# One core, six sweeps over a 4096x4096 matrix: another block order in the first sweep, 25 blocks taken whole in place of 32, small work at other places

## The chip, the cores and the metric

One core of a Trainium2 chip runs the whole program. The metric is device time in microseconds from the start to the end of one execution; lower is better. The engines that matter here are TensorE (PE in the profile; PEld is its weight load), VectorE (DVE), ScalarE (ACT), GpSimd (POOL) and SyncE (SP), which only issues transfers.

## The reference, cut to what matters

Six products with the same adjacency matrix `adj` (4096x4096, float32), each between small work on rows of 128 values:

```python
def ref_cut(x, adj, ...):
    deg = clip(sum(adj, axis=1), 1.0)
    x = layernorm(x + x @ W_self + (adj @ x / deg) @ W_neigh)        # sweep 0
    x = layernorm(x + relu(adj @ (x @ kernel) + bias))               # sweep 1
    h = relu(adj @ (x @ W1) + b1)                                    # sweep 2
    x = layernorm(x + relu(adj @ (h @ W2) + b2))                     # sweep 3
    x1 = silu((adj @ x) @ W + b)                                     # sweep 4
    return layernorm(x + silu((adj @ x1) @ W + b))                   # sweep 5
```

## The kernel before

**Tiling.** `adj` is cut into 8x8 blocks of 512x512. A block (r, k) comes in two tiles of 128x1024 float32 (512 KB each); each tile is one *step* of the program. `STEPS` lists them in their order: 516 steps, of which 0 to 129 and a few after are of the first sweep. The step is loaded by SP into one of six buffers `raw` (L434). Use of a step by TensorE is a *product*; `PRODUCTS` lists 768 of them. A product adds into `acc`, a bank of PSUM for one of the 48 sums (`FINISH` numbers the sums m = 0 to 47 in the order in which they end, 8 for each sweep; FINAL is 47).

**Two ways through TensorE.** A *whole* step (`whole_step`, L476) multiplies the raw float32 tile: each float32 matmul of 512 columns is two records in the profile, four records for a step. A *split* step (`split_step`) needs two rounded parts first. ScalarE writes `adj_hi` (a rounding of the tile, L729), VectorE writes `adj_lo` = raw - `adj_hi` (L882), and TensorE does six single-pass matmuls: L488 and L489 twice on `adj_hi`, then L493 twice on `adj_lo`. The operand (`op_hi`, `op_lo`) is split likewise. Parts lie in nine slots (`SPLIT`), with four more in the last sweep, in the space of `op_hi` and `op_lo` of the sweep before; so there the same L729 and L882 write `op_hi` and `op_lo`. A split step can serve two sweeps from one load: in the order table, WHOLE is a whole block, ONE a split block used for one sweep, BOTH for two sweeps at once, and FIRST with a later SECOND for two sweeps at two places. 

**Degrees.** In the first sweep VectorE also adds every tile of `adj` into `deg_part` (L751 for the first pair of a row of blocks, L754 after it), and each sum waits for the one before it, since it reads it. At a row's end it makes `deg_sum` (L759). A raw buffer of a whole step is free for the next load when TensorE and the degree sum have read it; that of a split step when `adj_lo` and the degree sum are made.

**Small work of the first sweep,** for each sum m. TensorE: `degrees` (L511) puts the row sums across partitions, `rows_of_x` (L503) makes x @ (W_self + I), `times_weight` (L525) multiplies the finished sum by the weight. VectorE: L807 and L809 clip and invert the degree (`rdeg`; L807 waits for L511), L813 to L770 add and take means and variances (ending in `var_eps`), L847 makes `shift`, L865 the next operand's `op_lo`. GpSimd computes `rstd` = var_eps ** -0.5 (L905) between `var_eps` and `shift`. ScalarE: `sum_out` (L612) copies the finished bank to `t_agg`, L663 scales, L683 normalises into `t_x`, L692 makes `op_hi`.

**In the last sweep,** VectorE adds the bias (L829, waits for L525), ScalarE applies silu (L674), VectorE adds the residual and takes the moments (L842 to L770), GpSimd and L847 follow, ScalarE normalises (L683) and issues the store (L704). The last two steps are worked off in `last_block` (L562, L564, L569) with smaller pieces and a short chain to the end (L619, L537, L632, L780, L909, L797).

**What sets the order.** Nothing is scheduled at run time. Each engine walks through its own list in program order and blocks at a semaphore that is not there yet. The block order is the table `FIRST_ORDER` (and tables for the later sweeps). The place of each piece of small work is a number in a second set of tables. For TensorE (`ROWS_AT`, `DEGREES_AT`, `WEIGHT_AT`) it is the number of the product that it stands before. For ScalarE and VectorE (`SUM_AT`, `NORM_AT`, `SCALE_AT`, `RESIDUAL_AT` and others) it is eight times a step plus a part: a number u stands before the split of step u // 8. An operation that stands early blocks whatever is behind it on its engine.

Of the kernel before, what the change touches and what calls it, by code (L numbers as in the profile page):

```python
# [5 lines left out]
def bass_gnn_residual_norm_kernel(  # L6
# [52 lines left out]
        (0, 1, 0, WHOLE), (0, 0, 0, WHOLE), (0, 1, 1, WHOLE), (0, 0, 1, WHOLE), (0, 1, 5, WHOLE), (0, 0, 7, WHOLE),  # L59
        (0, 0, 5, WHOLE), (0, 1, 4, WHOLE), (0, 0, 4, WHOLE), (0, 0, 3, WHOLE), (0, 0, 6, WHOLE), (0, 0, 2, WHOLE),  # L60
        (0, 1, 2, WHOLE), (0, 1, 3, ONE), (0, 2, 5, WHOLE), (0, 1, 6, WHOLE), (0, 1, 7, WHOLE), (0, 2, 2, WHOLE),
        (0, 2, 6, WHOLE), (0, 2, 3, ONE), (0, 2, 7, WHOLE), (0, 3, 5, WHOLE), (0, 2, 1, WHOLE), (0, 2, 4, WHOLE),
        (0, 2, 0, BOTH), (0, 3, 6, WHOLE), (0, 3, 1, BOTH), (0, 4, 0, BOTH), (0, 4, 4, WHOLE), (0, 3, 2, BOTH),
        (0, 3, 3, ONE), (0, 4, 7, WHOLE), (0, 3, 0, BOTH), (0, 3, 4, ONE), (0, 3, 7, WHOLE), (0, 4, 1, BOTH),
        (0, 5, 0, FIRST), (0, 5, 6, WHOLE), (0, 4, 2, BOTH), (0, 4, 5, WHOLE), (0, 5, 2, BOTH), (0, 4, 3, BOTH),
        (0, 4, 6, WHOLE), (0, 5, 1, FIRST), (0, 5, 0, SECOND), (0, 5, 4, FIRST), (0, 6, 2, FIRST), (0, 5, 1, SECOND),
# [4 lines left out]
        (1, 3, 3, ONE), (1, 2, 2, ONE), (0, 7, 6, SECOND), (0, 6, 5, SECOND)
# [92 lines left out]
    for s, g in enumerate(SPLIT_STEP):  # L164
# [778 lines left out]
```

## Time and profile before

| | |
|---|---|
| median of 3 runs | 1144.3 us (1143.35 to 1145.77) |
| profiled execution, its own time | 1143.78 us |
| its span, first to last instruction | 1141.7 us |
| TensorE busy | 1130.8 us, 99% |
| VectorE busy | 829.4 us, 73% |
| ScalarE busy | 571.9 us, 50% |
| DMA | 278.41 MB, mean 244 GB/s |

Between the span and the execution's own time lie 2.1 us of start and end. Engines run side by side, so their shares don't add up. Matmul records overlap: a record is longer than the distance to the next one. What an instruction costs its engine's queue is therefore read from the distance of two starts in the timeline, or from the chain of work, where each piece is counted from one release to the next.

### The profile page before, as it was taken

The page shows a single profiled execution, that of the slowest core. Times are in us where ns is not written, and L with a number is a line of the kernel's source. Part 1 is how long each engine was busy: PE and PEld are TensorE (multiplying, and loading weights), DVE is VectorE, ACT ScalarE, POOL GpSimd, SP SyncE. Part 2 cuts the span into 40 slices and gives each one's busy share as a digit, 9 for nine tenths or more (in the row PEclk, how much of TensorE's full clock was granted, in tenths as well). Part 3 has the DMA queues.
Part 4 walks back from the last instruction along what each step waited for, and adds up shares of the span by engine and source line. Part 5 has one row for each costly group of instructions (what it writes and reads, how often), then busy time and mean ns, then how long its engine had stood idle before and what let it go on. Part 6 is the DMA issues. An engine that isn't in the chain of part 4 may idle for free.

```text
span 1141.7 us, 14128 instructions
## 1 busy us (share of the span) xinstructions
PE 1130.8 (99%) x5012; PEld 901.1 (79%) x5012; DVE 829.4 (73%) x1089; ACT 571.9 (50%) x669; POOL 72.8 (6%) x49
## 2 busy tenths in 40 slices
PE   8999999999999999999999999999999999999997
PEld 3556677778888888888888888888888888888886
DVE  6898899889898666585544498566678455677887
ACT  1234335435754444474444474444467445566875
POOL 0010000000141111000000010000000000000121
PEclk9999999999999999999999999999999999999999
DMA  9988677666868666596656587666658665797885
GB/s 356 342 287 278 228 251 249 228 220 204 296 210 293 210 193 213 176 345 225 213 184 210 175 297 271 218 199 213 222 200 323 212 206 186 247 330 282 310 277 175
DMA packets 82643, 278.41 MB, mean 244 GB/s; under 512 B 8848, under 2 KB 14480, under 8 KB 82576
## 3 DMA queue, kind: packets, MB, share of 16 engines
q1 hardware_dynamic: 76144, 272.86, 69.7%
q10 hardware_dynamic: 6432, 4.65, 1.4%
q8 instruction: 42, 0.69, 0.2%
q14 instruction: 25, 0.20, 0.0%
HBM read 275.38 MB, written 2.10 MB: 243 GB/s over the span
## 4 chain that ended last, share of the span: by engine, by line
PE 96%; DVE 2%; DMA 1%; ACT 0%; issue 0%; SPq 0%; POOLq 0%; POOL 0%; ACTq 0%; DVEq 0%
PE acc L488 27%; PE acc L493 27%; PE acc L489 27%; PE acc L476 10%; PE acc L525 4%; DMA raw<-adj_tiles 1%; DVE adj_lo L882 1%; PE acc L503 1%; PE acc L511 1%; ACT adj_hi L729 0%; DVE stats L765 0%; ACT t_x L683 0%; DVE t_y L829 0%; DVE op_lo L882 0%; DVE x_rows L852 0%
## 5 line engine op out<-in xcount | busy, mean ns | idle before, releaser
L882 DVE TENSOR_TENSOR adj_lo<-raw,adj_hi 128x1024 fp32r<-128x1024 f32 x431 | 523.3, 1228 | 252.6 <-ACT adj_hi L729 237.2
L729 ACT CAST adj_hi<-raw 128x1024 fp32r<-128x1024 f32 x431 | 450.6, 1051 | 382.5 <-PE acc L493 271.1
L488 PE MATMUL acc<-adj_hi,op_hi 128*128 128x512 f32 x1360 | 537.3, 395 | 0.0
L489 PE MATMUL acc<-adj_hi,op_lo 128*128 128x512 f32 x1360 | 529.7, 390 | 0.0
L493 PE MATMUL acc<-adj_lo,op_hi 128*128 128x512 f32 x1360 | 419.1, 389 | 0.2 <-DVE adj_lo L882 0.2
L493 PEld LDWEIGHTS acc<-adj_lo,op_hi 128*128 128x128 f32 x1360 | 255.2, 188 | 54.2 <-DVE adj_lo L882 0.6
L489 PEld LDWEIGHTS acc<-adj_hi,op_lo 128*128 128x128 f32 x1360 | 255.6, 188 | 53.2 <-issue 1.9
L488 PEld LDWEIGHTS acc<-adj_hi,op_hi 128*128 128x128 f32 x1360 | 255.5, 188 | 53.2 <-issue 1.9
L754 DVE TENSOR_TENSOR deg_part<-deg_part,raw 128x1024 f32<-128x1024 f32 x112 | 136.8, 1222 | 7.0 <-DMA raw<-adj_tiles 3.8
L905 POOL TENSOR_TENSOR rstd<-var_eps,minus_half 128x4 f32<-128x4 f32 x31 | 55.2, 1782 | 1056.2 <-DVE var_eps L770 1056.2
L476 PE MATMUL acc<-raw,x_rows 128*128 128x512 f32 x256 | 115.1, 600 | 4.4 <-DMA x_rows<-x_blocks 4.2
L476 PEld LDWEIGHTS acc<-raw,x_rows 128*128 128x128 f32 x256 | 48.3, 192 | 58.7 <-issue 53.1
L612 ACT COPY t_agg<-acc 128x512 f32<-128x512 f32 x47 | 27.6, 586 | 83.6 <-PE acc L493 70.4
L882 DVE TENSOR_TENSOR op_lo<-raw,op_hi 128x1024 fp32r<-128x1024 f32 x21 | 25.4, 1223 | 12.5 <-ACT op_hi L729 12.1
L525 PEld LDWEIGHTS acc<-w,t_agg 128*128 128x128 f32 x248 | 32.4, 191 | 2.4
L525 PE MATMUL acc<-w,t_agg 128*128 128x128 f32 x248 | 32.6, 274 | 0.0
L683 ACT ACTIVATE t_x<-t_y,shift,rstd 128x128 f32<-128x128 f32 x60 | 24.7, 483 | 12.3 <-DVE shift L847 12.1
L729 ACT CAST op_hi<-raw 128x1024 fp32r<-128x1024 f32 x21 | 21.9, 1049 | 13.8 <-PE acc L493 8.6
L765 DVE BATCH_NORM_STATS2 stats<-t_y 128x6 f32<-128x128 f32 x124 | 27.1, 282 | 1.1
L829 DVE TENSOR_TENSOR t_y<-acc,b 128x512 f32<-128x512 f32 x31 | 21.3, 687 | 7.6 <-PE acc L525 7.6
L852 DVE TENSOR_SCALAR x_rows<-t_y,moments,rstd 128x128 f32<-128x128 f32 x64 | 21.6, 400 | 0.0
L604 ACT CAST op_hi<-x_rows 128x512 fp32r<-128x512 f32 x8 | 4.9, 619 | 29.1 <-DMA x_rows<-x_blocks 29.1
(70 smaller groups left out, 327.0 us busy)
## 6 DMA issues: line engine op xcount, KB each, us to landing
raw<-adj_tiles SPq DMA_DIRECT2D x515, 512.0 KB, 4.8
xt<-x_t ACTq DMA_DIRECT2D x8, 256.0 KB, 4.6
x_rows<-x_blocks SPq DMA_DIRECT2D x7, 256.0 KB, 6.3
out<-t_x ACTq DMA_DIRECT2D x7, 256.0 KB, 4.3
raw<-adj_tiles SPq DMA_DIRECT2D x2, 256.0 KB, 3.4
out<-xt SPq DMA_DIRECT2D x2, 128.0 KB, 2.1
x_rows<-x_blocks SPq DMA_DIRECT2D x1, 192.0 KB, 3.5
w<-W ACTq DMA_DIRECT2D x2, 64.0 KB, 3.3
```

The lines of the kernel that those rows point to most:

```text
L476: last = nc.tensor.matmul(bank, cols(x_rows, k)[:, j * P:(j + 1) * P], raw[:, g % RAW, b * CW:(b + 1) * CW], start=first and b == 0, stop= ...
L488: nc.tensor.matmul(bank, op_block(op_hi, p, j), a_hi, start=first and b == 0, stop=False)
L489: nc.tensor.matmul(bank, op_block(op_lo, p, j), a_hi, start=False, stop=False)
L493: last = nc.tensor.matmul(bank, op_block(op_hi, p, j), split_lo(s)[:, b * CW:(b + 1) * CW], start=False, stop=ends and b == BPT - 1)
L525: last = nc.tensor.matmul(bank[:, b * D:(b + 1) * D], t_agg[:, m % 2, b * P:(b + 1) * P], W_OF[p][:], start=True, stop=True)
L612: nc.scalar.copy(t_agg[:, m % 2, :], acc[:, BANK["sum", m], :]).then_inc(agg_out, 1)
L683: nc.scalar.activation(t_x[:, blk], t_y[:, m % 2, blk], ACT.Identity, bias=shift[:, m % 2, b:b + 1], scale=rstd[:, m % 2, b:b + 1]).then_i ...
L729: nc.scalar.copy(split_hi(s), raw[:, g % RAW, :]).then_inc(hi_ready, 1)
L754: nc.vector.tensor_tensor(sums, sums, src, ALU.add).then_inc(deg_step, 1)
L765: nc.vector.bn_stats(stats[:, m % 2, b, :], t_y[:, m % 2, b * D:(b + 1) * D]).then_inc(stats_ready, 1)
L882: nc.vector.tensor_tensor(split_lo(s), raw[:, g % RAW, :], split_hi(s).bitcast(fp32), ALU.subtract).then_inc(lo_ready, 1)
L905: nc.gpsimd.tensor_tensor(rstd[:, m % 2, :], var_eps[:, m % 2, :], minus_half[:], ALU.pow).then_inc(rstd_ready, 1)
```

## The change

Four things, all in tables; no function is touched.

1. `FIRST_ORDER` is another order of the first sweep's blocks, with 25 blocks WHOLE in place of 32. The other seven are split: 14 steps more, 466 in place of 452. The number of steps (516) and of products (768), and so the loads, stay; from step 134 and product 186 on the steps and products are the same ones.
2. The places of the first sweep's small work follow the new order.
3. In the sweeps between, some small work moves by one or two steps.
4. In the last sweep, bias, residual and moments of most sums stand one to five steps later, and around the end the order on ScalarE and VectorE is another.

The first and last lines of the tables that the prediction speaks of:

```diff
     FIRST_ORDER = [
-        (0, 1, 0, WHOLE), (0, 0, 0, WHOLE), (0, 1, 1, WHOLE), (0, 0, 1, WHOLE), (0, 1, 5, WHOLE), (0, 0, 7, WHOLE),
...
-        (1, 3, 3, ONE), (1, 2, 2, ONE), (0, 7, 6, SECOND), (0, 6, 5, SECOND)
+        (0, 0, 5, WHOLE), (0, 1, 5, WHOLE), (0, 0, 1, WHOLE), (0, 1, 1, WHOLE), (0, 0, 6, WHOLE), (0, 0, 3, WHOLE),
...
+        (0, 7, 6, SECOND)
     ]
...
     DEGREES_AT = [
-        25, 35, 52, 80, 103, 130, 150, 178
+        25, 33, 59, 75, 100, 136, 161, 179
     ]
...
     SUM_AT = [
...
-        3198, 3278, 3374, 3454, 3686, 3830, 3878, 3918, 3958, 3974, 4022, 4094, 4129
+        3198, 3278, 3374, 3454, 3686, 3830, 3878, 3926, 3974, 3998, 4054, 4128, 4131
     ]
     SCALE_AT = [
...
-        None, None, None, None, None, 3901, 3941, 3972, 4006, 4029, 4126, 4131
+        None, None, None, None, None, 3894, 3942, 3996, 4038, 4053, 4110, 4130
     ]
...
     NORM_AT = [
-        254, 334, 462, 630, 742, 894, 974, 1118, 1212, 1222, 1246, 1350, 1430, 1526, 1606, 1702, None, None,
+        238, 318, 518, 598, 726, 902, 1030, 1126, 1220, 1236, 1254, 1350, 1430, 1518, 1598, 1702, None, None,
...
     RESIDUAL_AT = 40 * [None] + [
-        3862, 3894, 3926, 3958, 3974, 4030, 4128, 4129
+        3854, 3902, 3950, 3990, 4006, 4070, 4129, 4131
     ]
```

**VectorE after the first sum of the first sweep, before** (from the moments of m = 0, behind step 27, to step 38; `deg_part` is the running row sum, `shift` waits for GpSimd's `rstd`):

```order
L768 BN_AGGR moments<-stats 128x2 x4
L770 TENSOR_SCALAR var_eps<-moments 128x4
L751 TENSOR_TENSOR deg_part<-raw 128x1024
L754 TENSOR_TENSOR deg_part<-deg_part,raw 128x1024
L847 SCALAR_TENSOR_TENSOR shift<-moments,rstd 128x4
L754 TENSOR_TENSOR deg_part<-deg_part,raw 128x1024 x3
L759 TENSOR_TENSOR deg_sum<-deg_part 128x512
L865 TENSOR_TENSOR op_lo<-t_x,op_hi 128x512
L754 TENSOR_TENSOR deg_part<-deg_part,raw 128x1024 x3
L807 TENSOR_SCALAR rdeg<-acc 128x4
```

The same place with the change (every line number is one higher, since the table is a line longer):

```order
L769 BN_AGGR moments<-stats 128x2 x4
L771 TENSOR_SCALAR var_eps<-moments 128x4
L755 TENSOR_TENSOR deg_part<-deg_part,raw 128x1024
L848 SCALAR_TENSOR_TENSOR shift<-moments,rstd 128x4
L755 TENSOR_TENSOR deg_part<-deg_part,raw 128x1024 x3
L760 TENSOR_TENSOR deg_sum<-deg_part 128x512
L866 TENSOR_TENSOR op_lo<-t_x,op_hi 128x512
L752 TENSOR_TENSOR deg_part<-raw 128x1024
L883 TENSOR_TENSOR adj_lo<-raw,adj_hi 128x1024
L808 TENSOR_SCALAR rdeg<-acc 128x4
```

What moved: between `var_eps` and `shift` stands one degree sum in place of two, and the next split comes four steps sooner.

**ScalarE at the end of the program, before** (the last four steps' splits; `t_agg<-acc 128x512` is the copy of the sum m = 46, `t_x` the normalisation, `128x256` the pieces of the last block):

```order
L612 COPY t_agg<-acc 128x512
L729 CAST op_hi<-raw 128x1024 x2
L729 CAST adj_hi<-raw 128x1024 x2
L683 ACTIVATE t_x<-t_y,shift,rstd 128x128 x4
L704 DMA out<-t_x 128x4x128
L729 CAST adj_hi<-raw 128x1024
L674 ACTIVATE t_aux<-t_y 128x512
L619 COPY t_agg<-acc 128x256 x2
L632 ACTIVATE t_aux<-acc 128x256
L624 COPY t_agg<-acc 128x256
L632 ACTIVATE t_aux<-acc 128x256
L683 ACTIVATE t_x<-t_y,shift,rstd 128x128 x4
```

With the change:

```order
L684 ACTIVATE t_x<-t_y,shift,rstd 128x128 x4
L705 DMA out<-t_x 128x4x128
L730 CAST adj_hi<-raw 128x1024 x3
L613 COPY t_agg<-acc 128x512
L675 ACTIVATE t_aux<-t_y 128x512
L684 ACTIVATE t_x<-t_y,shift,rstd 128x128 x4
L705 DMA out<-t_x 128x4x128
L620 COPY t_agg<-acc 128x256 x2
L633 ACTIVATE t_aux<-acc 128x256
L625 COPY t_agg<-acc 128x256
L633 ACTIVATE t_aux<-acc 128x256
```

What moved: the normalisation of m = 45 stands before the last three splits and no longer between them; the copy of m = 46 stands behind the last split in place of five splits ahead of it; the normalisation and store of m = 46 stand before the copies of the last sum and not at the very end. TensorE's order at the end did not change: its `times_weight` of m = 46, which waits for that copy, is still before product 762, six products from the end.

## Rows read from the trace of the kernel before

**Rows 1.** The page, parts 1 and 2: busy time of engines; TensorE's clock over the span.

```profile
PE 1130.8 (99%) x5012; PEld 901.1 (79%) x5012; DVE 829.4 (73%) x1089; ACT 571.9 (50%) x669; POOL 72.8 (6%) x49
...
PEclk9999999999999999999999999999999999999999
```

**Rows 2.** TensorE's waits from 320 us on: us in total, times, longest.

```profile
PE acc L569 <- DVE adj_lo L882: 0.5, 1, 0.5
PE acc L562 <- ACT adj_hi L729: 0.3, 1, 0.3
PE acc L493 <- DVE adj_lo L882: 0.2, 1, 0.2
```

**Rows 3.** The chain of work, 50 to 111 us: start, us, what.

```profile
50.21 0.79 PE acc L511 x8
51.00 1.82 PE acc L476 x4
52.82 0.89 PE acc L525 x8
...
56.03 0.45 PE acc L493 x2
...
83.39 10.30 PE acc L476 x24
...
108.00 0.45 PE acc L493 x2
...
109.36 0.45 PE acc L493 x2
```

**Rows 4.** VectorE's timeline, 51 to 58 us: start, us, engine, line, operation.

```profile
51.04 0.16 DVE L807 TENSOR_SCALAR rdeg<-acc 128x4 f32<-128x4 f32 x1 [3.79 <-PE acc L511]
...
51.33 1.20 DVE L882 TENSOR_TENSOR adj_lo<-raw,adj_hi 128x1024 fp32r<-128x1024 f32 x1
52.44 1.22 DVE L754 TENSOR_TENSOR deg_part<-deg_part,raw 128x1024 f32<-128x1024 f32 x1
53.58 1.22 DVE L882 TENSOR_TENSOR adj_lo<-raw,adj_hi 128x1024 fp32r<-128x1024 f32 x1
...
55.84 0.69 DVE L813 TENSOR_TENSOR t_y<-t_y,t_aux 128x512 f32<-128x512 f32 x1
...
57.89 0.17 DVE L770 TENSOR_SCALAR var_eps<-moments 128x4 f32<-128x4 f32 x1
```

**Rows 5.** VectorE's timeline, 60 to 66 us.

```profile
60.66 3.88 DVE L754 TENSOR_TENSOR deg_part<-deg_part,raw 128x1024 f32<-128x1024 f32 x3
64.57 0.69 DVE L759 TENSOR_TENSOR deg_sum<-deg_part 128x512 f32<-128x512 f32 x1
65.18 0.68 DVE L865 TENSOR_TENSOR op_lo<-t_x,op_hi 128x512 fp32r<-128x512 f32 x1
```

**Rows 6.** Timeline, 78 to 81 us: moments of m = 1, GpSimd, shift.

```profile
78.25 0.17 DVE L770 TENSOR_SCALAR var_eps<-moments 128x4 f32<-128x4 f32 x1
...
80.45 0.16 DVE L847 SCALAR_TENSOR_TENSOR shift<-moments,rstd 128x4 f32<-128x4 f32 x1 [0.90 <-POOL rstd L905]
```

**Rows 7.** VectorE's waits, 1065 to 1112 us: us in total, times, longest.

```profile
DVE t_y L829 <- PE acc L525: 3.5, 4, 1.5
DVE t_y L842 <- ACT t_aux L674: 2.3, 3, 1.0
```

**Rows 8.** Timeline of ScalarE at the end.

```profile
1120.69 0.59 ACT L612 COPY t_agg<-acc 128x512 f32<-128x512 f32 x1 [0.23 <-PE acc L493]
...
1127.45 1.65 ACT L683 ACTIVATE t_x<-t_y,shift,rstd 128x128 f32<-128x128 f32 x4
...
1129.61 1.05 ACT L729 CAST adj_hi<-raw 128x1024 fp32r<-128x1024 f32 x1 [0.51 <-ACT t_x L683]
...
1132.51 0.65 ACT L619 COPY t_agg<-acc 128x256 f32<-128x256 f32 x2 [1.32 <-PE acc L569]
```

**Rows 9.** Timeline of TensorE at the end.

```profile
1123.21 1.05 PE L525 MATMUL acc<-w,t_agg 128*128 128x128 f32 x8
```

More of the change, by code:

```diff
@@ L69, in bass_gnn_residual_norm_kernel @@
-        (0, 6, 1, FIRST), (0, 6, 7, WHOLE), (0, 6, 0, BOTH), (0, 7, 0, BOTH), (0, 6, 1, SECOND), (0, 6, 4, SECOND),
-        (0, 7, 3, BOTH), (0, 7, 5, BOTH), (0, 7, 6, FIRST), (0, 7, 7, ONE), (0, 7, 2, BOTH), (0, 7, 1, BOTH),
-        (1, 3, 3, ONE), (1, 2, 2, ONE), (0, 7, 6, SECOND), (0, 6, 5, SECOND)
+        (0, 0, 5, WHOLE), (0, 1, 5, WHOLE), (0, 0, 1, WHOLE), (0, 1, 1, WHOLE), (0, 0, 6, WHOLE), (0, 0, 3, WHOLE),
+        (0, 1, 3, WHOLE), (0, 1, 6, WHOLE), (0, 0, 2, WHOLE), (0, 0, 4, WHOLE), (0, 0, 0, WHOLE), (0, 0, 7, WHOLE),
@@ new lines, in bass_gnn_residual_norm_kernel @@
+        (0, 1, 4, WHOLE), (0, 1, 7, ONE), (0, 1, 0, WHOLE), (0, 1, 2, WHOLE), (0, 2, 3, WHOLE), (0, 3, 3, ONE),
+        (0, 3, 7, WHOLE), (0, 2, 7, WHOLE), (0, 2, 5, ONE), (0, 2, 1, WHOLE), (0, 2, 4, ONE), (0, 2, 6, WHOLE),
+        (0, 3, 5, WHOLE), (0, 2, 2, WHOLE), (0, 3, 1, BOTH), (0, 2, 0, BOTH), (0, 3, 6, ONE), (0, 4, 4, WHOLE),
+        (0, 3, 4, ONE), (0, 3, 0, BOTH), (0, 4, 5, WHOLE), (0, 3, 2, BOTH), (0, 4, 1, BOTH), (0, 4, 7, ONE),
+        (0, 4, 6, WHOLE), (0, 5, 5, ONE), (0, 4, 0, BOTH), (0, 4, 2, BOTH), (0, 5, 0, FIRST), (0, 4, 3, BOTH),
@@ new lines, in bass_gnn_residual_norm_kernel @@
+        (0, 5, 3, FIRST), (0, 5, 0, SECOND), (0, 6, 2, BOTH), (0, 6, 3, FIRST), (0, 5, 1, BOTH), (0, 5, 4, BOTH),
+        (0, 6, 4, FIRST), (0, 5, 3, SECOND), (0, 5, 2, BOTH), (0, 5, 6, ONE), (0, 6, 1, FIRST), (1, 4, 4, ONE),
+        (0, 5, 7, ONE), (0, 6, 4, SECOND), (0, 6, 3, SECOND), (0, 6, 7, ONE), (0, 7, 2, FIRST), (0, 7, 3, FIRST),
+        (0, 6, 1, SECOND), (0, 6, 0, FIRST), (0, 7, 2, SECOND), (0, 7, 3, SECOND), (0, 6, 6, ONE), (0, 7, 0, BOTH),
+        (0, 6, 5, FIRST), (0, 7, 4, FIRST), (0, 6, 5, SECOND), (0, 7, 7, ONE), (0, 7, 5, BOTH), (0, 7, 1, FIRST),
@@ L72, in bass_gnn_residual_norm_kernel @@
+        (0, 6, 0, SECOND), (1, 2, 2, ONE), (0, 7, 6, FIRST), (0, 7, 1, SECOND), (0, 7, 4, SECOND), (1, 3, 3, ONE),
+        (0, 7, 6, SECOND)
     ]
@@ L174, in bass_gnn_residual_norm_kernel @@
     ROWS_AT = [
-        21, 31, 42, 59, 88, 111, 138, 158
+        21, 31, 39, 66, 82, 108, 143, 168
     ]
     DEGREES_AT = [
-        25, 35, 52, 80, 103, 130, 150, 178
+        25, 33, 59, 75, 100, 136, 161, 179
     ]
     WEIGHT_AT = [
-        26, 37, 54, 83, 106, 133, 153, 180, 194, 198, 202, 220, 238, 260, 278, 304, 318, 322, 326, 348, 366,
-        388, 406, 432, 446, 450, 454, 476, 494, 516, 534, 560, 574, 578, 582, 604, 622, 644, 662, 702, 720, 726,
-        732, 738, 742, 750, 762, 768
+        26, 34, 61, 77, 103, 138, 163, 181, 194, 198, 202, 220, 238, 260, 278, 304, 318, 322, 326, 348, 366,
+        388, 406, 432, 446, 450, 454, 476, 494, 516, 534, 560, 574, 579, 582, 604, 622, 644, 662, 702, 720, 726,
+        732, 738, 742, 751, 762, 768
     ]
```

31 lines of the change are left out of this document (11 added, 20 removed), and 16 rows, old and new, of tables (BIAS_AT, NORM_AT, SCALE_AT, SUM_AT).

## The prediction, made before the changed kernel ran

> **What bounds the kernel now.** I read the page's busy shares first. TensorE is busy 99% of the span and its clock stands at full speed (2.4 GHz) throughout [rows 1]. Then the waits: from 320 us to the end TensorE waits 1.0 us in all, 0.8 us of it at the last block [rows 2], and in the first sweep only for its first operands. So TensorE's own work sets the time, almost everywhere. What shortens that work shortens the kernel, as long as no wait appears in its place. The question is whether VectorE, which pays for the exchange, can keep up in the first sweep.
>
> **What a step costs TensorE.** In the chain, 24 records of whole matmuls, six steps, take 10.30 us: 1.717 us a step [rows 3]. A split step is the distance between two L493 pairs in a row, 109.36 - 108.00 = 1.36 us [rows 3]; 1.361 over longer runs. A step that goes from whole to split saves 0.356 us. Fourteen do: **14 x 0.356 = 5.0 us** less on TensorE. Small matmuls are as many as before. Loads are as many as before.
>
> **What a step costs VectorE.** A split adds one `adj_lo` for each step. The records say 1.22 us, but starts lie closer: `adj_lo` at 51.33, a degree sum at 52.44, `adj_lo` at 53.58 [rows 4], so 1.13 us is what the queue pays for an `adj_lo` or a degree sum where the two alternate. Three degree sums in a row take 3.88 us with the last one's 1.22 in it, 1.33 from start to start [rows 5], since each reads the one before. Moments of one m, from L813 to L770, are 57.89 - 55.84 = 2.05 us [rows 4]. `deg_sum` is 0.61 from start to start, and `op_lo` with a record of the same length as much [rows 5], the `rdeg` pair 0.29 [rows 4], `shift` under 0.1.
>
> The Trainium skill, VectorE: DVE Perf Modes, section The DRAIN you can't avoid, says that the next operation does not start until the pipe of the one before is empty. By that rule each of these costs its full record, about 0.09 us more. The starts just quoted show otherwise here, but the rule is a rival below, because it would turn this change's sign.
>
> **The first sweep, term by term.** VectorE's last forced stop in the early part is at L807 for m = 0, which waits for TensorE's degrees: it starts at 51.04 us, and TensorE ended them at 51.00 [rows 3, 4]. All this stays in place with the change, because the first 26 steps are whole in both orders and degrees stay before product 25. From there I count both queues up to each split, without any waits, and take the difference: how early is `adj_lo` when TensorE wants it. On the kernel before this gives 1.2 us at step 27; traced, `adj_lo` starts at 53.58 and ends at 54.80, and its L493 begins at 56.03 in the chain, 1.2 us as well [rows 3, 4]. It is a count by program order, one engine against the other.
>
> With the change the tightest place is step 45. VectorE has before it 7 `adj_lo` and 17 degree sums (24 x 1.134 = 27.2), nine places where a degree sum follows another or `deg_sum` follows one (1.5), two moments (4.1), two `rdeg` pairs (0.6), two `op_lo`, a `deg_sum` and two `shift` (2.0): 35.4 us. So `adj_lo` of step 45 starts at 86.4 and ends at 87.65. TensorE has 13 whole and 7 split steps (22.3 + 9.5) and five pieces of small work at 0.79 and 0.89 [rows 3] (4.35; L503 taken like L525, both four matmuls of one size), and 0.25 for turning from degrees or weights to the next step (the pair behind L511 takes 1.82, not 1.72 [rows 3]): it reaches step 45 at 87.45 and its L493 0.91 later, 88.36. That is 0.7 us to spare, 0.65 after the 0.05 of a semaphore.
>
> But one stop is not in that count. `shift` of m = 0 now stands one degree sum behind `var_eps`. Where the kernel before has this spacing, for m = 1, GpSimd is too late: `var_eps` at 78.25, `shift` at 80.45, with 0.90 us of idle time [rows 6]. From start to start that is 2.20 us where the queue alone would need 1.2, so 1.0 us is lost; before, m = 0 had two sums in between and nothing was lost. All that follows on VectorE moves back 1.0 us, with nothing else idle before step 45 to absorb it: `adj_lo` comes 0.35 us too late there. TensorE waits **about 0.4 us** at that step. Bounds: 0 if my two sums are off by 0.4 of some 36 us, and 1.0 if another stop is added.
>
> Behind that the same count leaves, after the 1.0 and with TensorE 0.4 later, 0.4 to 0.6 us at steps 53 and 63, 0.9 at 77 and 83, 1.4 at 105 (there a slot comes free late and ScalarE's and VectorE's splits follow it), 2 or more at 111 and after. VectorE has 181 us of work for the 184 us from 51 us to step 111: it is a second bound, 98% full, and any further idle microsecond in it before step 83 costs TensorE in full. From step 132 on it is 10 us early and the rest is as before.
>
> **The sweeps between** change by a step or two at places where TensorE waits 0.2 us in all [rows 2]: nothing.
>
> **The end.** Before, the last split on ScalarE stood behind the normalisation of m = 45, whose four pieces and store issue filled 1127.45 to 1129.6, so it started at 1129.61 [rows 8] and TensorE waited 0.8 us for it and for `adj_lo` [rows 2]. Now that split stands early. In its place ScalarE has m = 46 before the last sum's copies. Its chain: weights end at 1124.1 (1123.21 [rows 9] and 0.9), bias and silu 0.7 each, like L813 of their size [rows 4], moments 2.05 [rows 4], GpSimd and shift 2.2 [rows 6], normalisation 1.65 and store issue to the next start 0.5 [rows 8], semaphores 0.2: the copy L619 can start at 1132.1, where it started at 1132.51 [rows 8]. The end gains **0.3 us** and not 0.8. Bounds: 0 and 0.8.
>
> **Sum.** 1143.8 (the profiled execution's own time) - 5.0 + 0.4 - 0.3 = 1138.9 us. That execution lies 0.5 us under the median of the three runs, so by a median it is 1138.9 to 1139.4; I take 1139.1. A measurement of this kernel can tell about 0.2%, 2.3 us, from no change.
>
> **Rivals.**
> *VectorE becomes the bound* (2 in 10). Between steps 45 and 83 loads or ScalarE's splits come late by another 1 to 3 us, which VectorE can't make up. For: the count leaves under 1 us at five steps, and before the change VectorE was not as full and could be late at no cost. Against: a buffer that VectorE frees is wanted by it again only five steps later, 11 us at two operations a step. TensorE then waits 1.5 to 4 us: 1140 to 1143, middle 1141.5.
>
> *The copy of m = 46 comes too late: slower* (6 in 100). It stands behind the last split, and TensorE's L525 before product 762 waits for it, at 1123.21 in the time of before [rows 8, 9]. If the last split stayed where it is now, ending at 1130.7, the copy would end at 1131.3 and TensorE would stand for 8.2 us: 1143.8 - 5.0 + 8.2 - 0.8 = 1146.2. The new kernel is slower from the point where that split ends later than about 1127.4. Against: the last loads wait for buffers that VectorE frees, and VectorE stood 5.8 us in that stretch before sums and silus that were not ready [rows 7]; now they stand one to five steps later and most of this falls away. I put the last split's end near 1120.5, 2 us before it is wanted.
>
> *The records' lengths are the cost* (1 in 100). VectorE's 138 large operations up to step 111, less some 25 already spaced by the sums, would each take 0.09 more, 10 us; less the 2 to 3 to spare TensorE waits 7.5: 1146.4. The page named above would have it so; rows 4 speak against it.
>
> *No wait at all* (15 in 100): the stop at `shift` is absorbed; 1138.5, or 1138.0 with all of 0.8 at the end. It differs little from my forecast.
>
> **How the numbers follow.** Forecast 58 in 100, no wait 15, VectorE bound 20, copy late 6, lengths 1. The likeliest alone spans 1138.2 to 1140.0. For 8 in 10 I go to 1137.8 below and to 1142.0 above, which takes in most of the VectorE rival. Faster by over 0.2% means under 1142.0: forecast, no wait, and 14 of the 20; 0.86 with rounding. Within 0.2%: 0.08. Slower: 0.06.
>
> **What would show it.** The profile after: 200 whole matmul records (L477) in place of 256; TensorE busy near 1126; idle of about 1 us at L848 near 59 us, and TensorE waiting for `adj_lo` once, around 88 us, by 0.2 to 0.7; VectorE with hardly any idle time between 51 and 285 us; no wait at L525 near 1118; the last split on ScalarE well before TensorE wants it. I am wrong if TensorE waits for `adj_lo` at several places between 88 and 235 us, or for ScalarE's copy at the end.

## The result, and the profile after

The kernel before took 1144.5 us in the median and the changed one 1142.2 (1139.8 to 1145.9): ratio 0.9979, interval 0.9972 to 0.9987. It is faster, by 2.3 us, half of the 5 that were forecast, and just outside the range on record. In that comparison the changed kernel's times spread over 6 us and those of before over 2.7. Over all comparisons the kernel before has a median of 1144.0 (1142.6 to 1146.8, 108 executions).

The head of the page of the changed kernel, whose profiled execution took 1142.3 us by its own time:

```profile
span 1140.2 us, 14213 instructions
PE 1128.1 (99%) x5040; PEld 906.2 (79%) x5040; DVE 843.9 (74%) x1103; ACT 585.4 (51%) x683; POOL 70.2 (6%) x49
PEclk9999999999999999999999999999999999999999
```

TensorE is busy 2.7 us less than before [rows 1], not 5. What it waited for up to 320 us (above the dots), and from there to the end (below):

```profile
PE acc L477 <- DMA x_rows<-x_blocks: 4.9, 2, 3.9
PE acc L489 <- ACT adj_hi L730: 0.2, 1, 0.2
PE acc L494 <- DVE adj_lo L883: 0.2, 1, 0.2
...
PE acc L526 <- ACT t_agg L613: 1.2, 2, 0.9
```

Two things are new against [rows 2]: a wait for the copies of the sums (L613) in the last sweep, and none in the last block. The waits of VectorE from 50 to 286 us:

```profile
DVE rdeg L808 <- PE acc L512: 3.0, 1, 3.0
DVE adj_lo L883 <- ACT adj_hi L730: 2.2, 2, 1.5
DVE shift L848 <- POOL rstd L906: 0.9, 1, 0.9
DVE op_lo L866 <- ACT op_hi L693: 0.6, 1, 0.6
```

The waits don't add up to the time lost, since matmul records stretch over a short one. So I read lateness instead: the start of a product's first record, less what stands ahead of it at the prediction's prices (1.717 us a whole step, 1.361 a split one, 0.89 or 0.79 a piece of small work). Where that number stays, TensorE runs at full pace; where it grows, time is lost. It reads alike in all kernels, whatever their order. A "piece of small work" is one of the short matmul groups `degrees` (0.79), `rows_of_x` and `times_weight` (0.89 each). "End" is the time from the start of product 765 to the end of the span. Where a number of the experiments is called lateness, it is worked out in this way from the trace of the kernel named.

```
product      before  before_look  after  again  after_look
2              6.24      6.40      8.36   6.72     6.74
27             6.37      6.53      8.49   6.85     6.87
46             6.50      6.64      9.91   8.37     8.80
186            7.70      7.84     11.23   9.72    10.13
750            8.86      9.05     12.02  10.51    10.91
765            9.00      9.19     13.82  10.57    11.41
end           13.49     12.43     12.18  12.18    12.18
```

(before and before_look are two executions of the kernel before; after, again and after_look three of the changed one.) From the counts alone the changed kernel is 4.98 us shorter: 5.0 as forecast. Against that the first pair differs by +2.12 at the start, +1.29 between products 27 and 46 (1.42 against 0.13), +0.12 up to 186, -0.37 up to 750, +1.66 up to 765 and -1.31 at the end. With the 4.98 that is -1.47, and the spans differ by -1.5. The execution called again gives +0.48, +1.39, +0.15, -0.37, -0.08, -1.31: -4.72. So the same kernel landed at 1142.3 once and at 1139.3 once. The start and the last sweep differ from one execution to the next; the loss before product 46 is there each time (1.42, 1.52 and 1.93 us). The -0.37 is a gain that was not forecast. It lies in the sweeps between: from product 300 to 600 lateness grows by 0.43 to 0.54 us in the eleven executions that have the new places there, and by 0.88 to 0.93 in the five that have the old ones (the kernels warm and combined_warm left out).

### The profile page after: what moved, and what is told of

Its sections match the earlier page's. It is cut to its first block, busy times and chain, and to the rows that moved or that the text cites. A ratio compares the mean times of both kernels' runs of the same rounds, so it can differ in the third digit from the quotient of the medians.

```text
span 1140.2 us, 14213 instructions
## 1 busy us (share of the span) xinstructions
PE 1128.1 (99%) x5040; PEld 906.2 (79%) x5040; DVE 843.9 (74%) x1103; ACT 585.4 (51%) x683; POOL 70.2 (6%) x49
## 4 chain that ended last, share of the span: by engine, by line
PE 94%; DVE 2%; DMA 2%; ACT 1%; issue 1%; SPq 0%; POOLq 0%; POOL 0%; ACTq 0%; DVEq 0%
PE acc L489 28%; PE acc L494 28%; PE acc L490 28%; PE acc L477 7%; PE acc L526 4%; DMA raw<-adj_tiles 1%; DVE adj_lo L883 1%; PE acc L504 1%; PE acc L512 0%; DMA x_rows<-x_blocks 0%; DVE deg_part L755 0%; ACT t_x L684 0%; DVE deg_part L752 0%; ACT adj_hi L730 0%; DVE op_lo L883 0%
## 5 line engine op out<-in xcount | busy, mean ns | idle before, releaser
L883 DVE TENSOR_TENSOR adj_lo<-raw,adj_hi 128x1024 fp32r<-128x1024 f32 x445 | 540.4, 1228 | 243.3 <-ACT adj_hi L730 228.5
L730 ACT CAST adj_hi<-raw 128x1024 fp32r<-128x1024 f32 x445 | 465.2, 1051 | 384.0 <-PE acc L494 294.4
L489 PE MATMUL acc<-adj_hi,op_hi 128*128 128x512 f32 x1388 | 547.8, 395 | 0.2 <-ACT adj_hi L730 0.2
L490 PE MATMUL acc<-adj_hi,op_lo 128*128 128x512 f32 x1388 | 540.7, 390 | 0.0
L494 PE MATMUL acc<-adj_lo,op_hi 128*128 128x512 f32 x1388 | 427.9, 389 | 0.2 <-DVE adj_lo L883 0.2
L494 PEld LDWEIGHTS acc<-adj_lo,op_hi 128*128 128x128 f32 x1388 | 260.3, 188 | 55.9 <-DVE adj_lo L883 1.3
L489 PEld LDWEIGHTS acc<-adj_hi,op_hi 128*128 128x128 f32 x1388 | 260.8, 188 | 54.5 <-issue 2.0
L490 PEld LDWEIGHTS acc<-adj_hi,op_lo 128*128 128x128 f32 x1388 | 260.8, 188 | 53.7 <-issue 1.4
L477 PE MATMUL acc<-raw,x_rows 128*128 128x512 f32 x200 | 91.5, 610 | 4.9 <-DMA x_rows<-x_blocks 4.9
L477 PEld LDWEIGHTS acc<-raw,x_rows 128*128 128x128 f32 x200 | 38.3, 195 | 49.5 <-issue 42.5
L613 ACT COPY t_agg<-acc 128x512 f32<-128x512 f32 x47 | 27.5, 585 | 64.6 <-PE acc L494 59.2
L684 ACT ACTIVATE t_x<-t_y,shift,rstd 128x128 f32<-128x128 f32 x60 | 24.7, 483 | 9.4 <-DVE shift L848 9.4
```

The costliest lines, as they stand in the source:

```text
L477: last = nc.tensor.matmul(bank, cols(x_rows, k)[:, j * P:(j + 1) * P], raw[:, g % RAW, b * CW:(b + 1) * CW], start=first and b == 0, stop= ...
L489: nc.tensor.matmul(bank, op_block(op_hi, p, j), a_hi, start=first and b == 0, stop=False)
L490: nc.tensor.matmul(bank, op_block(op_lo, p, j), a_hi, start=False, stop=False)
L494: last = nc.tensor.matmul(bank, op_block(op_hi, p, j), split_lo(s)[:, b * CW:(b + 1) * CW], start=False, stop=ends and b == BPT - 1)
L613: nc.scalar.copy(t_agg[:, m % 2, :], acc[:, BANK["sum", m], :]).then_inc(agg_out, 1)
L684: nc.scalar.activation(t_x[:, blk], t_y[:, m % 2, blk], ACT.Identity, bias=shift[:, m % 2, b:b + 1], scale=rstd[:, m % 2, b:b + 1]).then_i ...
```

## The experiments

### Is the late start the order's doing?

```profile
3.94 2.08 PE L477 MATMUL acc<-raw,x_rows 128*128 128x512 f32 x2 [3.94 <-DMA x_rows<-x_blocks]
7.01 6.67 PE L477 MATMUL acc<-raw,x_rows 128*128 128x512 f32 x10 [0.99 <-DMA x_rows<-x_blocks]
```

This is TensorE's start in the changed kernel: after one matmul it stands until the rest of x has landed, at 7.01 us. In the kernel before that was at 5.25. The next runs take the changed kernel once more, and exchange columns or rows of the first blocks (all whole, so every engine keeps its list).

> The changed kernel once more, unchanged. In its profiled execution the first load of x landed at 7.01 us (before: 5.25) and every product from the second on stood 2.1 us later than in the kernel before. Theory A (that time varies from execution to execution, whatever the order): the profile shows a first product at 5 to 7 us and the times fall in two clusters about 2.2 us apart, as in the 14 executions so far (1139.8 to 1140.3 and 1141.5 to 1143.7), and the kernel before shows the same two clusters. Theory B (it lies in the new order's first loads): the profile shows 7.0 us again, and most times lie near 1142.

```diff
-        (0, 0, 5, WHOLE), (0, 1, 5, WHOLE), (0, 0, 1, WHOLE), ...
+        (0, 0, 0, WHOLE), (0, 1, 0, WHOLE), (0, 0, 1, WHOLE), ...     # col0
+        (0, 1, 5, WHOLE), (0, 0, 5, WHOLE), (0, 0, 1, WHOLE), ...     # row1
```

> The changed kernel with columns 5 and 0 exchanged in rows 0 and 1 of the first sweep, so that column 0 of x and of the matrix is loaded first, as in the kernel before; all four blocks are whole, so every engine's list stays the same. Theory B1 (the start of 2.1 us hangs on which column is loaded first): the first load of x lands near 5.3 us, median 1140.1. Theory A (variation) or B2 (the row first loaded, or anything behind the first blocks): as the changed kernel, 1142.2.

> The changed kernel with blocks (0, 0, 5) and (0, 1, 5) exchanged, so that row 1 comes first, as in the kernel before, but column 5 stays. Theory B2 (the row first loaded sets the start): x lands near 5.3 us, median 1140.1. Theories A and B1: as the changed kernel, 1142.2.

In before_col5 the blocks with columns 0 and 5 of the first two rows are exchanged in the order of before.

> The kernel before with columns 0 and 5 exchanged in rows 0 and 1 of the first sweep: column 5 is loaded first, all else as in the kernel before. Theory B1: the first load of x lands near 7.0 us and the median is 2.1 us above the kernel before, 1146.6. Theories A and B2: no difference, 1144.5.

Measured: again 1141.5 (1139.2 to 1144.8), ratio 0.9975 [0.9963, 0.9987]; col0 1142.1, 0.9980 [0.9971, 0.9989]; row1 1140.5, 0.9971 [0.9962, 0.9980]; before_col5 1143.9, 1.0001 [0.9992, 1.0011]. Lateness of product 2: 6.72, 8.66, 8.91, 6.20. The same kernel started at 8.36 in one execution and 6.72 in the other, and row1, with a start of 8.91 in its profile (that execution took 1143.8), had nine others from 1139.3 to 1141.2. Neither column nor row sets it.

Later, the first four blocks were exchanged between the two kernels as a whole.

```diff
# start_as_before
-        (0, 0, 5, WHOLE), (0, 1, 5, WHOLE), (0, 0, 1, WHOLE), (0, 1, 1, WHOLE), ...
+        (0, 1, 0, WHOLE), (0, 0, 0, WHOLE), (0, 1, 1, WHOLE), (0, 0, 1, WHOLE), ...
# before_new_start: the reverse, in the kernel before
```

> The changed kernel with its first four blocks those of the kernel before, in their order (all whole, the three that move exchanged with whole blocks of the same rows). If the start is chance: product 2 less two steps anywhere from 6.2 to 9.0 us, median as the changed kernel, 1141.8. If it hangs on the first blocks: 6.2 to 6.8 us and a median of 1140.8, 1 us lower.

> The kernel before with the first four blocks of the changed kernel. If the start is chance: median as the kernel before, 1144.0, and the start anywhere from 6.2 to 9.0 us. If it hangs on the first blocks: a start of 7 to 9 us, median 1 us over the kernel before.

> The kernel before, one more look. If the start is chance it may lie anywhere from 6.2 to 9.0 us; if it hangs on the first blocks it is 6.2 to 6.8.

> The changed kernel, one more look. Start from 6.5 to 9.0 us by either theory; 1.3 to 2.0 us lost between steps 41 and 46; 0 to 3 us lost at the last weights.

Measured: start_as_before 1141.5, ratio 0.9981 [0.9972, 0.9989], as the changed kernel; before_new_start 1144.3, 1.0004 [0.9995, 1.0013], as the kernel before. Starts: 7.57, 7.42, 6.40 (before_look, 1142.9 us) and 6.74 (after_look, 1139.9 us). So the first four blocks do not set it. That it is chance does not follow, since everything behind these blocks stayed as it was in each kernel. Grouped by that, the profiles differ: the five with the first sweep of before, rest_only below among them with 6.76, start at 6.2 to 7.4 us, 6.6 in the mean, and the eleven with the new one at 6.5 to 8.9, 7.6 in the mean (warm and combined_warm left out). One microsecond of the start may well belong to the order, or to the program as a whole.

What makes a start late can be seen in the weight loads, one for each matmul of 512 columns. The changed kernel:

```profile
9.73 0.34 PEld L477 LDWEIGHTS acc<-raw,x_rows 128*128 128x128 f32 x1 [0.52 <-issue]
10.59 0.34 PEld L477 LDWEIGHTS acc<-raw,x_rows 128*128 128x128 f32 x1 [0.52 <-issue]
11.37 0.19 PEld L477 LDWEIGHTS acc<-raw,x_rows 128*128 128x128 f32 x1 [0.45 <-issue]
11.80 0.19 PEld L477 LDWEIGHTS acc<-raw,x_rows 128*128 128x128 f32 x1 [0.24 <-issue]
```

And the kernel before:

```profile
5.25 0.34 PEld L476 LDWEIGHTS acc<-raw,x_rows 128*128 128x128 f32 x1 [0.52 <-DMA x_rows<-x_blocks]
6.11 0.34 PEld L476 LDWEIGHTS acc<-raw,x_rows 128*128 128x128 f32 x1 [0.52 <-issue]
7.85 0.30 PEld L476 LDWEIGHTS acc<-raw,x_rows 128*128 128x128 f32 x2 [1.41 <-issue]
8.39 0.19 PEld L476 LDWEIGHTS acc<-raw,x_rows 128*128 128x128 f32 x1 [0.24 <-issue]
8.82 0.19 PEld L476 LDWEIGHTS acc<-raw,x_rows 128*128 128x128 f32 x1 [0.24 <-issue]
```

At first the matmuls lie 0.86 us apart, and then 0.43. The change comes before 8 us in the kernel before, and at 11.3 us in the changed one, where TensorE had stood until 7.01 us.
```
                   x landed   full clock   lateness of product 2
before                 5.20         7.32          6.24
rest_only              5.30         8.36          6.76
before_new_start       5.40        10.05          7.42
again                  5.68         9.05          6.72
after                  6.96        11.29          8.36
col0                   5.56        13.36          8.66
row1                   7.01        13.04          8.91
```

In the main, the later the full clock, the later the start. In col0, row1 and mend_first below, where it came after 12 us, 0.3 to 0.8 us more were lost between products 2 and 27. The landing of x does not fix it: again and col0 have x at nearly the same time, and the clock 4.3 us apart. But the landing itself goes with the kernel: 5.0 to 5.4 us in all five executions with the first sweep of before, 5.5 to 7.0 in all thirteen with the new one (warm and combined_warm with them). It was 6.51 in start_as_before, although all loads issued until then are those of the kernel before. What in the new kernel delays it is open.

The kernel warm keeps TensorE busy with useless matmuls from 1.5 us on.

```diff
+            def warm(n):
+                for _ in range(n):
+                    nc.tensor.matmul(acc[:, 7, 0:P], ident[:], ident[:], start=True, stop=True)
...
                 if g == 0:
+                    pe.wait_ge(ident_ready, 1)
+                    warm(6)
                     pe.wait_ge(x_first_loaded, 16)
...
                 for b in range(BPT):
+                    if g == 0 and b == 1:
+                        warm(4)
+                    if g == 1 and b == 0:
+                        warm(2)
```

> The changed kernel with matmuls ahead that do nothing useful: TensorE multiplies the identity (128x128) by itself into an unused bank, six times before the first product, four between its first and second matmul, two before the second product, to be busy from 1.6 us on. In the profiles so far TensorE's matmuls start 0.86 us apart up to 7.9 us in the kernel before, up to 9.3 to 13.1 us in the new order, and 0.43 apart after. Theory (the slow pace ends after TensorE has been busy without a pause, and a late load of x puts this off): the matmuls of the products are 0.43 us apart from the first, product 2 starts by 9.6 us, the spread of times shrinks and the median is 1.5 to 2.5 us under the changed kernel. Rival (the start is lost to the loads alone): product 2 stands at 9.6 to 12.3 us as before, no gain; or the added matmuls delay the first product by 0.5 us or more.

Measured: 1141.7 (1139.4 to 1144.2), ratio 0.9982 [0.9973, 0.9991]; no gain. Its profile has a start of 6.95, within the range of the others. The full clock begins at 7.02 us there and at 5.50 in combined_warm below, earlier than in any of the sixteen kernels and executions without added matmuls (7.06 to 13.36), so they seem to bring it forward; two profiles are few to say so. Tile 1 landed only at 8.2 us (before: 7.7), and the last added matmuls, which stand ahead of its product, ended at 8.66. So the loads and the added matmuls set what was left of the start.

### Which half of the change brings what?

first_only is the kernel before with `FIRST_ORDER` and the first sweep's places (the entries of m = 0 to 7) of the change; rest_only is the kernel before with all the others.

> The kernel before with the block order and the small work of the first sweep of the changed kernel; all later tables as before. Theory (three places: the start varies by itself, 1.3 to 2.0 us are lost between steps 41 and 46 each time, 0 to 3 us in the last sweep because copies and normalisation there stand late): TensorE saves 5.0 and loses about 1.5 at steps 41 to 46, nothing at the two weights of the last sweep (no wait at the line of times_weight), and the end takes 12.8 to 13.5 us from product 765 as in the kernel before; median 3 to 3.5 us under the kernel before. Rival (the last sweep's losses come from the arrival of loads, wherever the copies stand): waits of 1 to 2.6 us there in this kernel too, median 2.5 us under or less.

> The kernel before with only the later sweeps' tables of the changed kernel. Theory: the middle gains 0.4 to 0.6, the end 0.6 to 1.3 (12.2 us from product 765), and the weights of m = 45 and 46 lose 0 to 3 us, different in each execution; median 0 to 1 us under the kernel before. Rival (the last sweep of the changed kernel is simply better): 1.2 to 1.9 us under, always. The start is that of the kernel before: if the start is chance it lies anywhere between 6.2 and 9.3 us (time of product 2 less two steps), if it hangs on the order it is 6.2 again.

Measured: first_only **1140.9** (1139.4 to 1142.5), ratio 0.9976 [0.9967, 0.9985]; rest_only **1144.3** (1143.1 to 1150.1), ratio 1.0015 [1.0004, 1.0026]. first_only gains as much as the whole change, and the rest together gains nothing. Its interval lies just above 1, mostly by three executions of 1146.2, 1147.6 and 1150.1 us; the medians are 0.3 us apart. The waits of TensorE from 320 us, in first_only (line numbers 13 higher than in the changed kernel, 12 in rest_only):

```profile
PE acc L507 <- DVE adj_lo L896: 0.2, 1, 0.2
```

and in rest_only:

```profile
PE acc L538 <- ACT t_agg L625: 1.6, 1, 1.6
```

L538 is `times_weight`. Lateness from product 750 to 753 grows by 1.88 us in rest_only (8.98 to 10.86), by 0.12 in first_only. From product 750 to 765 lateness grows by 0.14 us in each of the seven executions with the last sweep of before, and by 0.06 to 1.90 in the ten with the new one as it is (1.1 in the mean). At the end the new one does gain: from product 765 it is 12.17 or 12.18 us in all eleven executions with the new last sweep, mend_tail below among them, and with that of before 12.19 or 12.20 in four and 12.43, 12.81 and 13.49 in three, depending on when the last splits were ready.

Where the last sweep loses time shows in row1, where TensorE waited 1.6 us for this copy. ScalarE there:

```profile
1102.54 1.06 ACT L730 CAST adj_hi<-raw 128x1024 fp32r<-128x1024 f32 x1 [0.28 <-DMA raw<-adj_tiles]
1105.54 1.66 ACT L684 ACTIVATE t_x<-t_y,shift,rstd 128x128 f32<-128x128 f32 x4 [1.95 <-DMA out<-t_x]
1107.22 0.41 ACTq L705 DMA_DIRECT2D out<-t_x  x1
1107.73 0.58 ACT L613 COPY t_agg<-acc 128x512 f32<-128x512 f32 x1 [0.53 <-ACT t_x L684]
```

The normalisation (L684) of m = 44 overwrites the one buffer `t_x` and waits 1.95 us until the store of the sum before, issued at 1100.72, has landed; in rest_only it waited 2.38, in again 0.16. The change had put it one place ahead of the copy of m = 45 (4053 against 4054), where before the copy came first (4022 against 4029). The store is not the only thing that can make this copy late: mend_first, of the next part, lost 1.4 us here with a wait of 0.21 for the store; its ScalarE had stood 1.39 us before a split whose load landed at 1094.6. The copy of m = 46 stands behind the last split. In the changed kernel's own profile:

```profile
1117.32 1.64 ACT L684 ACTIVATE t_x<-t_y,shift,rstd 128x128 f32<-128x128 f32 x4
...
1119.46 2.95 ACT L730 CAST adj_hi<-raw 128x1024 fp32r<-128x1024 f32 x3 [0.51 <-PE acc L494]
1122.31 0.58 ACT L613 COPY t_agg<-acc 128x512 f32<-128x512 f32 x1
1122.94 1.16 PE L526 MATMUL acc<-w,t_agg 128*128 128x128 f32 x8 [0.91 <-ACT t_agg L613]
```

mend_tail moves both copies.

```diff
 SUM_AT:   m = 45: 4054 -> 4046      m = 46: 4128 -> 4118
```

> The changed kernel with two numbers moved: the copy of m = 45 stands ahead of the normalisation of m = 44 (which waits for a store) and one split earlier, the copy of m = 46 ahead of the last split and no longer behind it. Theory (TensorE waits at the last weights because these copies stand behind work that waits for the store and for loads): 0 to 0.5 us lost at the two weights in place of 0 to 3, median 0.7 to 1 us under the changed kernel. Rival (it is the loads that come late in the last sweep): losses of 1 us and more stay, now as waits for adj_hi or adj_lo, and the median is the same.

Measured: 1140.3 (1138.4 to 1142.6), ratio 0.9971 [0.9961, 0.9980]; no wait at `times_weight`, and lateness from product 750 to 765 grows by 0.06 (11.23 to 11.29) in place of 1.80. Against the kernel before it is 3.1 us, where the changed kernel had 2.3 and 2.7. (Its profile lost 2.3 us between products 27 and 46, more than any other: there `op_lo` waited 1.52 us for `op_hi`.)

### What is lost between products 27 and 46?

VectorE in the changed kernel, `shift` of m = 0, and then `op_lo` of m = 1 up to the split of step 45:

```profile
60.01 0.17 DVE L771 TENSOR_SCALAR var_eps<-moments 128x4 f32<-128x4 f32 x1
60.09 1.23 DVE L755 TENSOR_TENSOR deg_part<-deg_part,raw 128x1024 f32<-128x1024 f32 x1
62.23 0.16 DVE L848 SCALAR_TENSOR_TENSOR shift<-moments,rstd 128x4 f32<-128x4 f32 x1 [0.91 <-POOL rstd L906]
...
82.43 0.69 DVE L866 TENSOR_TENSOR op_lo<-t_x,op_hi 128x512 fp32r<-128x512 f32 x1 [0.59 <-ACT op_hi L693]
83.04 1.22 DVE L883 TENSOR_TENSOR adj_lo<-raw,adj_hi 128x1024 fp32r<-128x1024 f32 x1
84.17 3.87 DVE L755 TENSOR_TENSOR deg_part<-deg_part,raw 128x1024 f32<-128x1024 f32 x3
87.97 1.22 DVE L883 TENSOR_TENSOR adj_lo<-raw,adj_hi 128x1024 fp32r<-128x1024 f32 x1
89.10 1.22 DVE L755 TENSOR_TENSOR deg_part<-deg_part,raw 128x1024 f32<-128x1024 f32 x1
90.24 1.22 DVE L883 TENSOR_TENSOR adj_lo<-raw,adj_hi 128x1024 fp32r<-128x1024 f32 x1
```

Two stops. The second was not in my count: `op_hi` of m = 1 stands on ScalarE behind the splits of steps 40 and 41, and the second of these waited for its load until 79.15 us. The load of step 45, for its part, took 6.9 us, since it was issued at 82.1 behind the load of transposed x at 81.86, and ScalarE could split it only at 88.97. So the question is whether VectorE or that load held TensorE up. ScalarE and its queue there:

```profile
79.15 1.05 ACT L730 CAST adj_hi<-raw 128x1024 fp32r<-128x1024 f32 x1 [0.71 <-DMA raw<-adj_tiles]
...
81.86 0.33 ACTq L711 DMA_DIRECT2D xt<-x_t  x1
...
88.97 1.05 ACT L730 CAST adj_hi<-raw 128x1024 fp32r<-128x1024 f32 x1 [4.00 <-DMA raw<-adj_tiles]
```

```diff
 NORM_AT:   m = 0: 238 -> 246                       # shift_later and mend_first
 SCALE_AT:  m = 1: 356 -> 330                       # mend_first
 OP_HI_AT:  m = 1: 357 -> 331                       # mend_first
 SELF_AT:   m = 2: 358 -> 374                       # mend_first
```

> The changed kernel with four numbers moved in the first sweep: shift of m = 0 one degree sum later, normalisation and op_hi of m = 1 ahead of the split of step 41 on ScalarE, and the copy that frees the transposed x (with the load behind it) after the loads of steps 45 and 46 are issued. Theory (VectorE's two stops of 0.9 and 0.6 us and the load of step 45 coming 1 us late behind the load of transposed x are what TensorE waits for): the 1.3 to 2.0 us lost between steps 41 and 46 fall to 0.4 or less; VectorE has no stop near 60 and 80 us; median 1.3 us under the changed kernel. Rival (VectorE and the DMA are full there whatever the places): 1 us or more is still lost at steps 41 to 53, median the same.

> The changed kernel with shift of m = 0 alone moved one degree sum later. VectorE has no stop near 60 us. Theory one bound (VectorE alone makes TensorE wait at steps 41 to 46): 0.9 us of the 1.3 to 2.0 lost there comes back. Theory two bounds (the load of step 45, queued behind the load of transposed x, comes as late as VectorE's adj_lo): 0.2 to 0.4 at steps 41 and 42 come back, the 1.1 us at steps 44 and 45 stay.

Measured: mend_first 1141.0 (1138.9 to 1142.3), ratio 0.9974 [0.9960, 0.9987], an interval too wide for a gain of 1 us; but lateness from product 27 to 46 grows by 0.15 us (9.05 to 9.20), as in the kernel before (0.13), and TensorE waits for nothing between 20 and 320 us. VectorE in mend_first:

```profile
60.56 0.17 DVE L774 TENSOR_SCALAR var_eps<-moments 128x4 f32<-128x4 f32 x1
60.64 2.55 DVE L758 TENSOR_TENSOR deg_part<-deg_part,raw 128x1024 f32<-128x1024 f32 x2
63.11 0.16 DVE L851 SCALAR_TENSOR_TENSOR shift<-moments,rstd 128x4 f32<-128x4 f32 x1
```

shift_later, one execution of 1139.3 us: growth 0.37 (7.24 to 7.61), where the three of the changed kernel have 1.42, 1.52 and 1.93. The second stop was 0.2 us there. So VectorE stopped 1.3 us less in all than in the first profile, and 1.05 to 1.56 came back. The load of step 45 landed at 86.8, 6.0 us after its issue, and cost nothing to speak of; but it had come earlier too, since VectorE frees its buffers, so this run alone does not tell the two apart. The profiles taken together do. VectorE's two stops against the growth of lateness from product 27 to 46, in us:

```
                  shift   op_lo   both   growth
mend_first            0       0      0     0.15
shift_later           0    0.24   0.24     0.37
first_only         0.91    0.15   1.06     0.97
row1               0.91    0.44   1.35     1.26
after              0.91    0.59   1.50     1.42
again              0.91    0.60   1.51     1.52
after_look         0.92    1.05   1.97     1.93
col0               0.91    1.10   2.01     2.02
start_as_before    0.92    1.09   2.01     2.10
mend_tail          0.91    1.52   2.43     2.34
```

What VectorE stands, TensorE loses, within 0.15 us. And the load is not what comes last: in after_look ScalarE split step 45 at 87.03 and was done at 88.08, and VectorE, which had no idle time there, took it up 1.05 us later, with 1.93 us lost. In first_only it was 1.5 us.

```profile
87.03 1.05 ACT L730 CAST adj_hi<-raw 128x1024 fp32r<-128x1024 f32 x1 [3.88 <-DMA raw<-adj_tiles]
89.13 1.22 DVE L883 TENSOR_TENSOR adj_lo<-raw,adj_hi 128x1024 fp32r<-128x1024 f32 x1
```

So VectorE's queue holds TensorE up. Loads come in one step earlier: they decide how long the second stop is, through the splits that `op_hi` stands behind.

### The parts together

combined: first sweep as in mend_first, the sweeps between as in the changed kernel, the last sweep (m = 40 to 47) as in the kernel before. combined_warm adds the useless matmuls, without the last two.

> First sweep of the changed kernel with the four numbers moved (as in the kernel mend_first), the sweeps between of the changed kernel, the last sweep's places of the kernel before. Theory (the parts add): against the kernel with the new first sweep alone (median 1140.9) 1.3 to 1.5 us less at steps 41 to 46 and 0.4 less in the middle: median 1139.2, lowest near 1137.5; no wait at the weights of the last sweep; what is left of the spread, some 3 us, is the start. Rival (what is mended is lost again later): median 1140.5 or more.

> The kernel combined with the useless matmuls ahead (six before the first product, four between its two matmuls, none before the second product). Theory (part of the start's spread is TensorE's slow pace, 0.86 us a matmul in place of 0.43, which goes on after a late x): the products' matmuls are 0.43 us apart from the second product on, product 2 starts 3.4 us behind product 1, the spread falls to 2 us and the median lies 0.5 to 1 us under that of combined. Rival (the loads alone set the start): median and spread as combined.

Measured: combined **1138.9** (1138.4 to 1140.4), ratio **0.9963** [0.9951, 0.9976]; combined_warm 1139.0 (1137.4 to 1140.6), 0.9963 [0.9950, 0.9975]. combined beats both kernels: 4.6 us under before in its comparison. In its profile TensorE waits for nothing from 14 us to the end, and lateness from product 27 to 46 grows by 0.48, with 0.25 us of stops on VectorE. The added matmuls bring nothing that can be measured. In combined_warm's profile TensorE waited 1.9 us at `times_weight` for copies in the middle sweeps (lateness 9.00 at product 300, 11.83 at 600), and 0.8 us in warm's; no profile of a kernel without added matmuls showed this. That is open.

## Why the prediction was off

**14 x 0.356 = 5.0 us off TensorE.** Right: 200 whole records, and the counts of the two kernels differ by 4.98 at these prices in the traces. What failed is what the sum set against it, 0.4 - 0.3 us, in three terms: the wait at step 45 was sized too small, and the start and the copies of the last sweep stood at nothing.

**"TensorE waits about 0.4 us" at step 45.** The mechanism was right, the size was not: lateness grew by 1.4 to 1.9 us in the three executions of the changed kernel, 0.13 before. VectorE's queue was counted well: from `rdeg` to `adj_lo` of step 45 I had 35.4 + 1.0 = 36.4 us, and it took 90.24 - 53.16 = 37.08. The 0.6 that are missing are the stop at `op_lo`, which I had left out: the kernel before has two of that kind in its first sweep, 1.1 us in all, where VectorE had time to spare. The forecast said that any further idle microsecond before step 83 costs TensorE in full, and so it did. The stop at `shift` was forecast at 1.0 and measured at 0.91. The place was right in part: lateness grows at steps 41, 44 and 45, between 83 and 92 us, and the count had put all of it at 45. Behind step 46 the count held: up to product 186 the changed kernel lost 0.1 us more than the kernel before, and the rival "VectorE becomes the bound" in its form of late places at steps 45 to 83 did not come.

**"All this stays in place with the change."** The sum built on the one profiled execution of before, at 1143.8, as if its start were the kernel's. Lateness of product 2 was 6.2 to 7.4 us in executions with the first sweep of before, 6.5 to 8.9 in those with the new one, 1.0 more in the mean. The execution that I built on had one of the earliest (6.24). That was worth 2.1 us in the first pair, and 0.5 in the next. The three times of before hinted at it, 1143.35 to 1145.77; I read this as a spread of the measurement and not as a term of the sum. And "its clock stands at full speed throughout" was a wrong reading of [rows 1]: up to 7.3 us the trace has no entry, and the matmuls ran at half pace.

**The copies of the last sweep.** "The copy of m = 46 comes too late" had 6 in 100. In the small this rival came true in the first profile: TensorE waited 0.9 us for that copy. I had put the last split's end 2 us before it is wanted, from loads that come on time; it was 0.9 late. Worse, I looked at this copy alone. The same tables put the copy of m = 45 behind a normalisation that waits for a store, and this cost 0.3 us more there and up to 1.9 (rest_only, row1). The sum had nothing for either.

**"The sweeps between ... nothing."** They gain 0.45 us.

**"The end gains 0.3 us."** The gain was 1.3 in the first pair, since the profiled execution of before had an end of 13.5 us. Against the mean of the seven executions with the old places, 12.5, it is the 0.3 that was forecast, but by luck. The chain of m = 46 was taken 0.9 us too long: from `var_eps` to `shift` it takes 1.29 us there and not 2.2, because `rstd` of this m takes 1.0 us in place of 1.9. The trace of before had that number too.

```profile
1127.58 0.17 DVE L771 TENSOR_SCALAR var_eps<-moments 128x4 f32<-128x4 f32 x1
1128.87 0.16 DVE L848 SCALAR_TENSOR_TENSOR shift<-moments,rstd 128x4 f32<-128x4 f32 x1 [1.12 <-POOL rstd L906]
```

**The records' lengths** as the price are out. The rival took them from the Trainium skill, VectorE: DVE Perf Modes, The DRAIN you can't avoid, and took its rule too strictly: the same paragraph goes on that an operation that is not held starts earlier. The trace agrees with that: where `adj_lo` and degree sums alternate they start 1.13 us apart again (87.97, 89.10, 90.24) with records of 1.22, and the count by starts was right to 0.1 us once the second stop is in it.

Had the first pair been again and before_look, the difference of the spans would have been 3.9 us. The median difference is 2.3 in one comparison and 2.7 in the next. An estimate from the means of all profiles comes near: -5.0 by the counts, +1.0 at the start, +1.6 up to product 46, +0.9 in the last sweep, -0.45 between and -0.3 at the end make about -2.2. My interval of 1137.8 to 1142.0 left out a case in which several small losses come together, none of them large.

## What to carry to other kernels

Before a sum is built on one profiled execution, split its time into the part that the program fixes and the part that differs from one execution to the next (the start, the arrival of loads and stores): the second belongs in the range, even if its trace looks settled.
## What the runs showed of the hardware beyond that

How long a store to DRAM takes to be seen as landed varies between executions in the same stretch full of loads: under 2.5 us in the changed kernel (issued at 1100.62, the next normalisation ran unhindered at 1103.08), 4.8 in row1 (1100.72 to 1105.54) and 5.0 in rest_only (1101.29 to 1106.31). TensorE's first matmuls ran at half pace, 0.86 us in place of 0.43, until the full clock came, at 7.1 us at the earliest and 13.4 at the latest without added matmuls. GpSimd's `rstd` of four values for each partition took 1.9 us most times and 1.0 at some places, for m = 46 each time. And waits of TensorE are understated where they are short: 0.4 us were listed in the first sweep behind the start, and lateness grew by 1.4.
